# An audio tower on Trainium2: six of the 32 products of a group's states with C on GpSimd instead of VectorE

## The chip, the cores and the metric

One core of a Trainium2 chip runs the whole program. The metric is the device time of one execution in microseconds (us). The engines are TensorE (PE, its weight loads shown as PEld), VectorE (DVE), ScalarE (ACT), GpSimd (POOL) and SyncE (SP, which issues most DMAs). Each takes its own list of instructions in order, and they meet at semaphores only.

## The reference, cut to what matters

The input is 64 sequences of 2 x 4096. A convolution and a projection make h of 64 x 128 tokens x 256; then comes a selective state-space layer on the normalized h, then a mixture of 8 experts, two for each token. The layer, with 512 inner channels d and 16 states n:

```python
xc = silu(conv(x_inner) + conv_b); x_ssm = xc @ W_xproj   # delta_raw, Bm, Cm
delta = softplus(delta_raw * w_dt + b_dt)
dA = exp(delta[..., None] * A)
dBx = delta[..., None] * Bm[:, :, None, :] * xc[..., None]
h = dA_t * h + dBx_t                 # over the 128 tokens of a sequence
y = einsum('bdn,bn->bd', h, c_t)     # states times C, summed over n
y = (y + xc * D_param) * silu(z); out = y @ W_out
```

Everything is computed in float32.

## The kernel before

The 64 sequences are worked in 16 groups of GB = 4, so a tile row has GT = 512 tokens. The 512 inner channels are NCH = 4 chunks of 128 partitions. A group is HU = 32 steps k; step k treats chunk k // 8 and the two states 2 (k % 8) and the next, as one tile of 128 x 1024. The groups run in `steps`: two unrolled, then a loop over pairs (two halves, `par` 0 and 1), then two unrolled. Each engine has a `step` function, whose order over k is written out by hand. After the groups comes the expert part, 136 tiles.

What a step does:
- ACT, `exps` (L726 and L732): writes dA = exp(delta A) into one of two PSUM pairs, `dA[k % 2]`. It may do so when the product of step k - 2 is done. ACT issues the exponentials of step k + 1 in step k, and after them the other work of that step: copies of z (L713), `norm1` of the next group (L655, at k = 3), copies for the next group's input projection and convolution (L667, L675), silu, softplus and others.
- POOL, `make_dbx` (L536): one multiply of 128 x 2048 for two steps, u times B, into one of two buffers. It may start when the scans of the buffer's previous content are done. In between come delta, u, small work for the normalizations (`rsqrt`) and scatters of rows.
- DVE, `scan` (L927): runs the recurrence in place in PSUM over `dA[k % 2]` and dBx. `times_c` (L935): multiplies the states with C (`c_rep`, in SBUF) into one of two SBUF buffers `hc[k % 2]`. In some steps come `gate_y`, `residual`, statistics and the router's small operations.
- PE, `add_state` (L1244): adds the two states' products into the chunk's PSUM bank `yacc` by two matmuls with the identity, after the other matmuls that `step` gives this k. These are the projection of z (k = 0 to 3), the output projection of the former group (`project_out`, L1256, k = 4 to 7), the input projection of the next group (`project_x`, L1190, k = 7, 10, 13, 16) and its convolution in two halves (`conv`, L1215, k = 8 and 9, 11 and 12, 14 and 15, 17 and 18), the small projection to delta, B and C (`x_ssm`, k = 20), transposes, the router, and the embedding of the group after next (`embed`, k = 24 and 25).
- SP: loads B and C of the next group in quarters as the old ones become free, saves `hnew` to DRAM (`save_h`) and loads it back into `hres` for the residual.

Three SBUF tensors of 128 x 1024 matter for the change. `hnew` holds the embedded h of the next group from step 25 until `norm1` has read it at step 3 and `save_h` has stored it. `hres` holds the former group's h from its load at the group's start to `residual` at step 9, and the transposed input (`xt`) at steps 22 to 25. `xn` holds the normalized h from step 3 to the transposes at steps 5 and 6, and the router's input at steps 14 to 16.

Of the kernel before, what the change touches and what calls it, by code (L numbers as in the profile page):

```python
# [5 lines left out]
ALU = mybir.AluOpType  # L6
# [11 lines left out]
def audio_tower(nc, x, W_embed, b_embed, W_proj, b_proj, W_in, conv_w, conv_b, W_xproj, w_dt, b_dt, A_log,  # L18
# [40 lines left out]
    with ExitStack() as ctx:  # L59
# [110 lines left out]
        emb_pair = [bank_a, bank_b]  # L170

        def scratch(i):
            return bank_b[:, (2 + i) * GB * E:(3 + i) * GB * E].rearrange("p (b e) -> p b e", b=GB)
# [61 lines left out]
        scan_done = sem("scan_done")  # L235
        hc_ready = sem("hc_ready")
        skip_done = sem("skip_done")
        sum_done = sem("sum_done")
# [87 lines left out]
        def _(sp):  # L326
# [25 lines left out]
            def load_hres(g, saves):  # L352

                sp.wait_ge(emb_full, 2 * saves)
                apart(sp, "sp")
                sp.wait_ge(h_saved, 16 * saves)
# [15 lines left out]
            def share_ssm(g):  # L372
# [10 lines left out]
                for q in range(NQ):  # L383
                    ahead(sp, dbx_ready, UN * (g - 1) + UN - NQ + q + 1)
                    apart(sp, "sp")
                    spread(flat(b_rep[:, q * QN:(q + 1) * QN, :]), g, 1 + q * QN, QN).then_inc(b_loaded[q], 16)
                    ahead(sp, hc_ready, HU * (g - 1) + HU - HC + 2 * q + 2)
                    apart(sp, "sp")
                    spread(flat(c_rep[:, q * QN:(q + 1) * QN, :]), g, 1 + S + q * QN, QN).then_inc(c_loaded[q], 16)

# [40 lines left out]
            def tail(g):  # L431
                load_hres(g, G)
                free_for(B_AT, (skip_done, NCH * G), (u_ready, NCH * G))
                free_for(C_AT, (dbx_ready, UN * G))
                free_for(C_AT + 2 * QN * GT, (hc_ready, HU * G - 4))
                free_for(X_AT + SCN, (hc_ready, HU * G), (scan_done, HU * G))
                free_for(E * MW)
                store_h2(g)
# [29 lines left out]
        def _(pool):  # L468
# [83 lines left out]
            def second_row(g):  # L552
# [4 lines left out]
                    .then_inc(second_set, 1)  # L557

            def scatter(g, k, b0):
                if b0 == 0:  # L560
# [67 lines left out]
        def _(actq):  # L628
# [7 lines left out]
            def evac_xt(g, m):  # L636
                actq.wait_ge(tx_full, 2 * g + m + 1)
                if m == 0:
                    ahead(actq, h2_ready, 2 * (g - 2))
                nc.scalar.activation(xt[m], bank_a[0:KX, :], ACT.Copy).then_inc(tx_free, 1)  # L640

            def evac_h(g, m):
                actq.wait_ge(emb_full, 2 * g + m + 1)
                if m == 0:
                    ahead(actq, h_saved, 16 * g)
                dst = hnew[:, 2 * m:2 * m + 2, :].rearrange("p b c -> p (b c)")
                nc.scalar.activation(dst, bank_a, ACT.Copy).then_inc(emb_free, 1)

            def norm1(g):

                actq.wait_ge(pow1, g + 1)
                ahead(actq, xnt_full, NK * g)
                ahead(actq, l_full, g - 2)
                for b in range(GB):
# [228 lines left out]
        def _(dve):  # L883
# [36 lines left out]
            def scan(g, k):  # L920
# [5 lines left out]
                src = flat(dBx[(k // 2) % 2][:, 2 * (k % 2):2 * (k % 2) + 2, :])  # L926
                nc.vector.tensor_tensor_scan(h, h, src, 0.0, ALU.mult, ALU.add).then_inc(scan_done, 1)  # L927

            def times_c(g, k):
                j = k % HC  # L930
                dve.wait_ge(scan_done, HU * g + k + 1)
                if k < HC and k % 2 == 0:
                    dve.wait_ge(c_loaded[k // 2], 16 * (g + 1))
                ahead(dve, sum_done, HU * g + k - 1)
                nc.vector.tensor_tensor(flat(hc[k % 2][:, :, :]), flat(dA[k % 2]), flat(c_rep[:, 2 * j:2 * j + 2, :]),  # L935
                                        ALU.mult).then_inc(hc_ready, 1)

            def gate_y(g, c):
                dve.wait_ge(sum_done, HU * g + HC * (c + 1))
                if c == 0:  # L940
# [204 lines left out]
        def _(pe):  # L1145
# [95 lines left out]
            def add_state(g, k):  # L1241
                pe.wait_ge(hc_ready, HU * g + k + 1)
                for i in range(2):
                    last = nc.tensor.matmul(yacc[(k // HC) % 2], ident[:, :], hc[k % 2][:, i, :], start=False,  # L1244
                                            stop=(k % HC == HC - 1 and i == 1))
                last.then_inc(sum_done, 1)
# [68 lines left out]
            def step(g, par, first, second, more, last):  # L1315
                for k in range(HU):
# [136 lines left out]
```

## Time and profile before

| | us |
|---|---|
| median of 3 runs | 3042.44 |
| lowest and highest | 3042.26, 3043.21 |
| the profiled execution | 3046.24 |
| its span, first to last instruction | 3044.5 |
| busy in it: PE, DVE, ACT, POOL | 2628.8, 2162.7, 1469.8, 1729.4 |

The profile is of one execution. The page gives each engine's busy time, then the span in 40 slices (76 us each; a digit is the busy share in tenths). A list of waits says which engine waited for which instruction's result. A timeline lists instructions in order of time: start, duration, engine, line, what is written and read; in brackets stands how long the engine was idle before, and who ended that. Lines are those of the kernel; `psum` in a row can be any of the PSUM banks, `arena` holds xc, B, C and dBx.

### The profile page before, as it was taken

To read this page: it belongs to the slowest core of one execution; us is meant where nothing else is said; L and a number is where in the kernel's file an instruction comes from. 1 tells how busy PE (TensorE), PEld (TensorE's weight loads), DVE (VectorE), ACT (ScalarE), POOL (GpSimd) and SP (SyncE) were. 2 spreads that over 40 slices of the span, in tenths; PEclk is the share of its full clock that TensorE was granted. 3 is DMA by queue.
4 is the path that set the end of the run, shared out by engine and by line. 5 is a ranking of instruction groups with operands and counts; after the bars stand their busy time and mean duration, and the time that the engine had idled before them with its cause. 6 is when DMAs were issued, how large, how long until landed. Compare 5 with 4: busy or idle time off the path is not lost. (4 is left out here: it accounts for less than half of the span.)

```text
span 3044.5 us, 32684 instructions
## 1 busy us (share of the span) xinstructions
PE 2628.8 (86%) x7774; PEld 1299.6 (43%) x7775; DVE 2162.7 (71%) x2367; ACT 1469.8 (48%) x2717; POOL 1729.4 (57%) x864
## 2 busy tenths in 40 slices
PE   4689898888979889897888978887569999999999
PEld 2234343343434334343333434333236666666665
DVE  0599999989999998998999999999632222222222
ACT  2565656656555665665666565665212222222222
POOL 1566767777685767768676676777422222222222
PEclk9899899999999999999999999999879999999999
DMA  1321303223040321303123140321432222222222
GB/s 38 126 101 37 144 27 134 78 75 131 21 145 27 132 92 60 140 16 141 56 103 117 36 144 26 132 86 64 165 80 44 43 45 44 44 44 44 45 44 31
DMA packets 125600, 235.91 MB, mean 77 GB/s; under 512 B 46449, under 2 KB 93714, under 8 KB 109122
## 3 DMA queue, kind: packets, MB, share of 16 engines
q1 hardware_dynamic: 98342, 200.56, 19.2%
q0 software_dynamic: 26128, 34.36, 6.5%
q14 instruction: 77, 0.63, 0.1%
q8 instruction: 17, 0.28, 0.0%
q10 hardware_dynamic: 1036, 0.09, 0.0%
HBM read 182.22 MB, written 53.78 MB: 78 GB/s over the span
## 5 line engine op out<-in xcount | busy, mean ns | idle before, releaser
L536 POOL TENSOR_TENSOR arena<-u,arena 128x2048 f32<-128x2048 f32 x256 | 1157.9, 4528 | 357.2 <-DVE psum L927 355.9
L1244 PE MATMUL psum<-hc,ident 128*128 128x512 f32 x2048 | 1060.8, 645 | 272.6 <-DVE hc L935 272.4
L927 DVE TENSOR_TENSOR_SCAN psum<-psum,arena 128x1024 f32<-128x1024 f32 x512 | 1172.9, 2291 | 124.4 <-ACT psum L732 83.2
L1244 PEld LDWEIGHTS psum<-hc,ident 128*128 128x128 f32 x2048 | 379.7, 200 | 836.6 <-DVE hc L935 485.5
L732 ACT ACTIVATE psum<-delta,a_neg 128x508 f32<-128x508 f32 x1024 | 656.4, 674 | 0.6
L935 DVE TENSOR_TENSOR hc<-psum,arena 128x1024 f32<-128x1024 f32 x512 | 626.0, 1223 | 19.9 <-DVE psum L927 4.8
L615 POOL DMA_INDIRECT out_dram<-hres,tok_id x136 | 211.1, 1552 | 599.4 <-ACT hres L864 550.0
L1375 PE MATMUL psum<-arena,xnt 128*128 x1088 | 516.0, 597 | 0.0
L1129 DVE COPY z<-psum 128x512 f32<-128x512 f32 x136 | 94.1, 692 | 458.0 <-PE psum L1384 458.0
L864 ACT ACTIVATE hres<-psum,tok_w 128x256 f32<-128x256 f32 x136 | 64.3, 473 | 454.4 <-PE psum L1394 447.7
L1394 PE MATMUL psum<-arena,z 128*128 x1088 | 257.1, 379 | 0.9 <-DVE z L1129 0.9
L1190 PE MATMUL psum<-xnt,w_in_sb 128*128 128x512 f32 x512 | 244.6, 601 | 3.1 <-ACT arena L675 1.6
L1394 PEld LDWEIGHTS psum<-arena,z 128*128 128x128 f32 x1088 | 206.6, 190 | 86.8 <-issue 65.7
L1375 PEld LDWEIGHTS psum<-arena,xnt 128*128 128x128 f32 x1088 | 186.5, 191 | 133.0 <-issue 132.0
L1215 PE MATMUL psum<-xi,diag_cw 128*128 128x512 f32 x512 | 239.8, 591 | 0.0
L726 ACT ACTIVATE psum<-zeros 128x8 f32<-128x8 f32 x512 | 87.8, 171 | 240.1 <-DVE hc L935 225.8
L1123 DVE TENSOR_TENSOR z<-psum,xn 128x512 f32<-128x512 f32 x136 | 94.1, 692 | 138.1 <-issue 98.2
L856 ACT ACTIVATE xn<-psum 128x512 f32<-128x512 f32 x136 | 81.2, 597 | 160.3 <-PE psum L1375 160.3
L1256 PE MATMUL psum<-w_out_sb,yz 128*128 128x256 f32 x512 | 129.0, 398 | 29.7 <-DVE h L953 28.9
L564 POOL DMA_INDIRECT expert_rows<-row,slot x128 | 130.0, 1015 | 39.6 <-issue 37.9
L1190 PEld LDWEIGHTS psum<-xnt,w_in_sb 128*128 128x128 f32 x512 | 98.4, 193 | 123.3 <-issue 119.4
L1215 PEld LDWEIGHTS psum<-xi,diag_cw 128*128 128x128 f32 x512 | 96.7, 189 | 123.0 <-issue 123.0
(145 smaller groups left out, 1921.4 us busy)
## 6 DMA issues: line engine op xcount, KB each, us to landing
arena<-ssm_rows SPq DMA_DIRECT2D x128, 1024.0 KB, 5.9
delta<-expert_rows SPq DMA_DIRECT2D x136, 129.0 KB, 2.0
h_saved_rows<-hnew SPq DMA_DIRECT2D x16, 512.0 KB, 6.5
hres<-h_saved_rows SPq DMA_DIRECT2D x16, 512.0 KB
out_dram<-h SPq DMA_DIRECT2D x16, 512.0 KB, 3.0
draw<-ssm_rows SPq DMA_DIRECT2D x16, 256.0 KB, 3.2
arena<-in_L_ffn_wg_dram SPq DMA_DIRECT2D x8, 512.0 KB
arena<-in_L_ffn_wi_dram SPq DMA_DIRECT2D x8, 512.0 KB
```

The source lines that it names most:

```text
L536: pool.tensor_tensor(dBx[k % 2], rep, b_rep[:, q * QN:(q + 1) * QN, :], ALU.mult).then_inc(dbx_ready, 1)
L564: pool.indirect_dma_start(out=rows_dram[:, :], out_offset=bass.IndirectOffsetOnAxis(ap=slot[:, k, b:b + 1], axis=0), in_=row[:, b, :], in_ ...
L615: pool.indirect_dma_start(out=out.rearrange("b o l -> (b o) l"), out_offset=bass.IndirectOffsetOnAxis(ap=tok_id[k][:, 0:1], axis=0), in_=y ...
L732: last = nc.scalar.activation(o, d, ACT.Exp, scale=a_neg[:, c, n:n + 1])
L927: nc.vector.tensor_tensor_scan(h, h, src, 0.0, ALU.mult, ALU.add).then_inc(scan_done, 1)
L935: nc.vector.tensor_tensor(flat(hc[k % 2][:, :, :]), flat(dA[k % 2]), flat(c_rep[:, 2 * j:2 * j + 2, :]), ALU.mult).then_inc(hc_ready, 1)
L1190: last = nc.tensor.matmul(dst, w_in_sb[:, k, c * P:(c + 1) * P], xnt[:, k, :], start=(k == 0), stop=(k == NK - 1))
L1215: last = nc.tensor.matmul(dst, diag_cw[:, c, k, :], xi[c % 2][:, :, k:k + T], start=(k == 0), stop=(k == TAPS - 1))
L1244: last = nc.tensor.matmul(yacc[(k // HC) % 2], ident[:, :], hc[k % 2][:, i, :], start=False, stop=(k % HC == HC - 1 and i == 1))
L1256: last = nc.tensor.matmul(bank_b[:, b * C:(b + 1) * C], yz[:, c, t0:t0 + T], w_out_sb[:, c, :], start=(c == 0), stop=(c == NCH - 1))
L1375: last = nc.tensor.matmul(dst[k % 2], xgt[k % 2][:, q * P:(q + 1) * P], w, start=(q == 0), stop=(q == NK - 1))
L1394: last = nc.tensor.matmul(py[k % 2], actt[k % 2][:, q * P:(q + 1) * P], w, start=(q == 0), stop=(q == NH - 1))
```

## The change

For the steps k = 4, 10, 12, 18, 20 and 26 of each group the scan writes its result into an SBUF tensor instead of PSUM (4, 10 and 18 into `hnew`, 12 into `hres`, 20 and 26 into `xn`), and GpSimd multiplies it there, in place, with C. The products of the other 26 steps stay on DVE. TensorE adds the product of one of the six steps later than before: 4 after 8, 10 after 14, 12 after 16, 18 after 22, 20 after 24, 26 after 30. GpSimd makes a product after the multiply of B numbered 4, 7, 8, 11, 12 and 15. DVE waits before such a scan until the tensor is free (`state_free`); ACT's exponentials may overwrite dA after the scan where the product is one of the six; ACT and SP get waits before they write the three tensors again. `rsqrt` of the second normalization moves from position 5 to 6 on GpSimd.

```diff
+        ON_POOL = {4: hnew, 10: hnew, 12: hres, 18: hnew, 20: xn, 26: xn}
+        DONE_WITH = {8: 4, 14: 10, 16: 12, 22: 18, 24: 20, 30: 26}
+        OWN = [k for k in range(HU) if k not in ON_POOL]
+        NOWN, NPL = len(OWN), len(ON_POOL)
+        SUMS = [k for own in OWN for k in ([own, DONE_WITH[own]] if own in DONE_WITH else [own])]
...
@@ SP: load_hres, share_ssm
+                sp.wait_ge(sum_done, HU * g + nth_sum[12] + 1)
...
+                    for k in (HU - HC + 2 * q, HU - HC + 2 * q + 1):
+                        if k in ON_POOL:
+                            ahead(sp, hc_pool, NPL * (g - 1) + nth_pool[k] + 1)
...
@@ POOL
+            def times_c(g, k):
+                pool.wait_ge(scan_done, HU * g + k + 1)
+                j = k % HC
+                if k < HC:
+                    pool.wait_ge(c_loaded[j // 2], 16 * (g + 1))
+                state = ON_POOL[k][:, :, :].rearrange("p b c -> p (b c)")
+                pool.tensor_tensor(state, state, flat(c_rep[:, 2 * j:2 * j + 2, :]), ALU.mult).then_inc(hc_pool, 1)
...
+                    if k in (4, 7, 8, 11, 12, 15):
+                        times_c(g, {4: 4, 7: 10, 8: 12, 11: 18, 12: 20, 15: 26}[k])
...
-                        if k == 5:
+                        if k == 6:
                             rsqrt(g - 1, 1, stat2, pow2)
@@ ACT: exps
-                ahead(actq, hc_ready, HU * g + k - 1)
+                if k >= 2 and k - 2 in ON_POOL:
+                    actq.wait_ge(scan_done, HU * g + k - 1)
+                elif k >= 2:
+                    actq.wait_ge(hc_ready, NOWN * g + nth_own[k - 2] + 1)
...
@@ DVE: scan
-                nc.vector.tensor_tensor_scan(h, h, src, 0.0, ALU.mult, ALU.add).then_inc(scan_done, 1)
+                if k in ON_POOL:
+                    state_free(g, k)
+                    out_ = ON_POOL[k][:, :, :].rearrange("p b c -> p (b c)")
+                else:
+                    out_ = h
+                nc.vector.tensor_tensor_scan(out_, h, src, 0.0, ALU.mult, ALU.add).then_inc(scan_done, 1)
+
+            def state_free(g, k):
+                known = isinstance(g, int)
+                if k == 4:
+                    dve.wait_ge(xn_ready, min(g + 2, G) if known else g + 2)
+                    dve.wait_ge(h_saved, 16 * (min(g + 2, G) if known else g + 2))
+                if k in (10, 18):
+                    dve.wait_ge(sum_done, HU * g + nth_sum[{10: 4, 18: 10}[k]] + 1)
+                if k == 12:
...
+                        dve.wait_ge(h2_ready, 2 * g)
+                if k == 20:
+                    dve.wait_ge(xnt_full, NK * (min(g + 2, G) if known else g + 2))
+                    ahead(dve, l_full, g)
+                if k == 26:
+                    dve.wait_ge(sum_done, HU * g + nth_sum[20] + 1)
...
             def times_c(g, k):
-                j = k % HC
+                if k in ON_POOL:
+                    return
...
@@ PE: add_state, step
-                pe.wait_ge(hc_ready, HU * g + k + 1)
+                if k in ON_POOL:
+                    pe.wait_ge(hc_pool, NPL * g + nth_pool[k] + 1)
...
-                    add_state(g, k)
+                    if k not in ON_POOL:
+                        add_state(g, k)
+                    if k in DONE_WITH:
+                        add_state(g, DONE_WITH[k])
```

## Rows read from the trace of the kernel before

**Rows 1.** The page, busy time by engine, and DVE in 40 slices of the span
```profile
PE 2628.8 (86%) x7774; PEld 1299.6 (43%) x7775; DVE 2162.7 (71%) x2367; ACT 1469.8 (48%) x2717; POOL 1729.4 (57%) x864
...
DVE  0599999989999998998999999999632222222222
```

**Rows 2.** Timeline of SP's DMA issues, the load of hres, two groups apart (start, duration)
```profile
759.54 0.34 SPq L358 DMA_DIRECT2D hres<-h_saved_rows  x1
...
1022.68 0.33 SPq L358 DMA_DIRECT2D hres<-h_saved_rows  x1
```

**Rows 3.** Waits from 300 to 2000 us, 13 groups: us in total, times, longest
```profile
POOL arena L536 <- DVE psum L927: 283.0, 114, 6.9
PE psum L1244 <- DVE hc L935: 189.5, 165, 2.5
...
ACT arena L675 <- PE psum L1215: 120.0, 39, 5.3
...
DVE psum L927 <- ACT psum L732: 72.9, 71, 2.7
```

**Rows 4.** One group in three windows: busy us of PE, PEld, DVE, ACT, POOL; clock; DMA
```profile
1015.00:1068.70 53.70, 50.46 (x137) 24.52 (x138) 49.16 (x40) 28.89 (x55) 43.15 (x21) 1.00 0.21 62
1068.70:1096.40 27.70, 27.70 (x83) 13.28 (x82) 26.95 (x27) 16.85 (x35) 18.21 (x5) 1.00 0.00 1
1096.40:1146.80 50.40, 35.56 (x86) 12.73 (x86) 45.61 (x47) 34.77 (x57) 34.70 (x23) 0.90 0.45 169
```

**Rows 5.** Instructions by line and form, 300 to 2000 us, GpSimd and DVE
```profile
L536 POOL TENSOR_TENSOR arena<-u,arena 128x2048 f32<-128x2048 f32 x208 | 940.8, 4528 | 284.1 <-DVE psum L927 283.0 <-issue 0.2
...
L520 POOL TENSOR_TENSOR delta<-delta,soft 128x512 f32<-128x512 f32 x52 | 66.0, 1269 | 2.4 <-ACT delta L707 2.4
...
L927 DVE TENSOR_TENSOR_SCAN psum<-psum,arena 128x1024 f32<-128x1024 f32 x415 | 950.9, 2291 | 92.8 <-ACT psum L732 72.9 <-issue 11.2 <-POOL arena L536 7.1
L935 DVE TENSOR_TENSOR hc<-psum,arena 128x1024 f32<-128x1024 f32 x416 | 508.7, 1223 | 16.9 <-DVE psum L927 4.8
```

**Rows 6.** Timeline of DVE: scan, product 4 and scan 5; scans 8, 14, 17, 21
```profile
1030.73 2.30 DVE L927 TENSOR_TENSOR_SCAN psum<-psum,arena 128x1024 f32<-128x1024 f32 x1 [0.77 <-POOL arena L536]
1033.06 1.22 DVE L935 TENSOR_TENSOR hc<-psum,arena 128x1024 f32<-128x1024 f32 x1
1034.21 2.29 DVE L927 TENSOR_TENSOR_SCAN psum<-psum,arena 128x1024 f32<-128x1024 f32 x1
...
1046.41 2.30 DVE L927 TENSOR_TENSOR_SCAN psum<-psum,arena 128x1024 f32<-128x1024 f32 x1 [1.06 <-ACT psum L732]
...
1071.93 2.30 DVE L927 TENSOR_TENSOR_SCAN psum<-psum,arena 128x1024 f32<-128x1024 f32 x1
...
1082.33 2.29 DVE L927 TENSOR_TENSOR_SCAN psum<-psum,arena 128x1024 f32<-128x1024 f32 x1
...
1100.93 2.30 DVE L927 TENSOR_TENSOR_SCAN psum<-psum,arena 128x1024 f32<-128x1024 f32 x1 [0.22 <-ACT psum L732]
```

**Rows 7.** Timeline of ACT: norm1, then the copies of convolutions 0 and 3
```profile
1030.79 2.06 ACT L655 ACTIVATE xn<-hnew,shift,rstd 128x256 f32<-128x256 f32 x4
...
1057.35 0.67 ACT L675 ACTIVATE arena<-psum,cb 128x512 f32<-128x512 f32 x1
...
1093.05 0.69 ACT L675 ACTIVATE arena<-psum,cb 128x512 f32<-128x512 f32 x1 [5.31 <-PE psum L1215]
```

**Rows 8.** Timeline of PE: a projection, convolutions 2 and 3, two sums
```profile
1041.94 1.99 PE L1256 MATMUL psum<-w_out_sb,yz 128*128 128x256 f32 x8 [1.73 <-DVE h L953]
...
1077.74 1.88 PE L1215 MATMUL psum<-xi,diag_cw 128*128 128x512 f32 x4
...
1091.13 1.88 PE L1215 MATMUL psum<-xi,diag_cw 128*128 128x512 f32 x4
1092.85 3.60 PE L1244 MATMUL psum<-hc,ident 128*128 128x512 f32 x8
```

**Rows 9.** Timeline of PE, the same projection in the group before
```profile
910.48 3.08 PE L1256 MATMUL psum<-w_out_sb,yz 128*128 128x256 f32 x8 [2.08 <-DVE h L953]
```

More of the change, by code:

```diff
@@ L170, in audio_tower @@
         emb_pair = [bank_a, bank_b]
+        ON_POOL = {4: hnew, 10: hnew, 12: hres, 18: hnew, 20: xn, 26: xn}
+        DONE_WITH = {8: 4, 14: 10, 16: 12, 22: 18, 24: 20, 30: 26}
+        OWN = [k for k in range(HU) if k not in ON_POOL]
+        NOWN, NPL = len(OWN), len(ON_POOL)
+        nth_own = {k: i for i, k in enumerate(OWN)}
+        nth_pool = {k: i for i, k in enumerate(ON_POOL)}
+        SUMS = [k for own in OWN for k in ([own, DONE_WITH[own]] if own in DONE_WITH else [own])]
+        nth_sum = {k: i for i, k in enumerate(SUMS)}
+        LAST_SUM = [max(nth_sum[k] for k in range(HC * c, HC * c + HC)) for c in range(NCH)]
+        assert len(SUMS) == HU and NOWN % 2 == 0 and not ON_POOL.keys() & {0, 1, HU - 2, HU - 1}
         def scratch(i):
@@ L386, in share_ssm @@
                     spread(flat(b_rep[:, q * QN:(q + 1) * QN, :]), g, 1 + q * QN, QN).then_inc(b_loaded[q], 16)
-                    ahead(sp, hc_ready, HU * (g - 1) + HU - HC + 2 * q + 2)
+                    last = [k for k in (HU - HC + 2 * q, HU - HC + 2 * q + 1) if k not in ON_POOL][-1]
+                    ahead(sp, hc_ready, NOWN * (g - 1) + nth_own[last] + 1)
                     apart(sp, "sp")
+                    for k in (HU - HC + 2 * q, HU - HC + 2 * q + 1):
+                        if k in ON_POOL:
+                            ahead(sp, hc_pool, NPL * (g - 1) + nth_pool[k] + 1)
+                            apart(sp, "sp")
                     spread(flat(c_rep[:, q * QN:(q + 1) * QN, :]), g, 1 + S + q * QN, QN).then_inc(c_loaded[q], 16)
@@ L639, in evac_xt @@
                     ahead(actq, h2_ready, 2 * (g - 2))
+                    ahead(actq, sum_done, HU * (g - 2) + nth_sum[12] + 1)
                 nc.scalar.activation(xt[m], bank_a[0:KX, :], ACT.Copy).then_inc(tx_free, 1)
@@ L645, in evac_h @@
                     ahead(actq, h_saved, 16 * g)
+                    ahead(actq, sum_done, HU * (g - 2) + nth_sum[18] + 1)
                 dst = hnew[:, 2 * m:2 * m + 2, :].rearrange("p b c -> p (b c)")
@@ L652, in norm1 @@
                 ahead(actq, xnt_full, NK * g)
+                ahead(actq, sum_done, HU * (g - 2) + nth_sum[26] + 1)
                 ahead(actq, l_full, g - 2)
@@ L929, in times_c @@
             def times_c(g, k):
[L930 removed]
+                if k in ON_POOL:
+                    return
+                j, n = k % HC, nth_own[k]
                 dve.wait_ge(scan_done, HU * g + k + 1)
[L932 removed]
+                if k < HC and (k % 2 == 0 or k - 1 in ON_POOL):
                     dve.wait_ge(c_loaded[k // 2], 16 * (g + 1))
[L934 to L935 removed]
+                if n >= 2:
+                    dve.wait_ge(sum_done, HU * g + nth_sum[OWN[n - 2]] + 1)
+                else:
+                    ahead(dve, sum_done, HU * (g - 1) + nth_sum[OWN[NOWN + n - 2]] + 1)
@@ L1241, in add_state @@
             def add_state(g, k):
-                pe.wait_ge(hc_ready, HU * g + k + 1)
+                if k in ON_POOL:
+                    pe.wait_ge(hc_pool, NPL * g + nth_pool[k] + 1)
+                    state = ON_POOL[k][:, :, :].rearrange("p (i b) c -> p i (b c)", i=2)
+                else:
+                    pe.wait_ge(hc_ready, NOWN * g + nth_own[k] + 1)
+                    state = hc[nth_own[k] % 2]
+                c = k // HC
                 for i in range(2):
-                    last = nc.tensor.matmul(yacc[(k // HC) % 2], ident[:, :], hc[k % 2][:, i, :], start=False,
-                                            stop=(k % HC == HC - 1 and i == 1))
+                    last = nc.tensor.matmul(yacc[c % 2], ident[:, :], state[:, i, :], start=False,
+                                            stop=(nth_sum[k] == LAST_SUM[c] and i == 1))
                 last.then_inc(sum_done, 1)
```

14 lines of the change are left out of this document (11 added, 3 removed).

## The prediction

> **What bounds the kernel now.** I read the page first: DVE is 9 or 10 tenths busy over the first 28 slices and 2 over the rest, where PE takes over with the expert tiles [rows 1]. The change lies wholly in the first part, 16 groups of 32 steps. Two groups take 263.14 us, 131.6 each [rows 2]. Then the waits of a stretch of 13 groups [rows 3]: PE waits 189.5 us for products of DVE, which looks as if DVE were the bound; but DVE itself waits 72.9 us for the exponentials of ACT, and ACT waits 120.0 us in its copies of the convolution for PE. So the three are one loop: ACT issues in order, exponentials (L732) stand behind copies out of PSUM (L675), and these wait for matmuls that stand in PE's order behind sums (L1244). Last, one group cut in three [rows 4]: in the middle, steps 12 to 20, PE is busy 27.70 us of 27.70, DVE 26.95. PE has idle time before and after it (3.2 of 53.7 and 14.8 of 50.4 us), none in it. That is what I weigh the change against.
>
> **What it takes off DVE.** A product costs 1.22 us, but the next scan starts 1.15 us after the product [rows 5, 6]. Six a group are 6.9 us, 110 us in 16 groups. The scan into SBUF in place of PSUM has no row; both the scan (PSUM out, 2291 ns for 1024 elements) and the product (SBUF out, 1223 ns) exist, and their ratio is that of the two operations, so I leave the scan at 2.29 us and allow 0.1 us either way, six times: 0.6 us a group.
>
> **What it puts on GpSimd.** 1024 elements between 512 in 1.27 us and 2048 in 4.53 us [rows 5]: 2.12 ns an element, 2.35 us (bounds 1.27 and 4.53). Six are 14.1 us a group. GpSimd waited 283.0 us for scans in 13 groups, 21.8 each [rows 3], so it fits; and it runs ahead: a product follows a multiply of B whose scans come later. The one place where it is close is dBx 8 behind product 10: GpSimd starts dBx 7 when scan 11 is done, and 4.5 + 2.35 + 4.5 us later dBx 8 is there, 4 us before scan 16. Product 26 stands ahead of the next group's delta, but that multiply waits for scan 29 anyway. The load of C's second quarter, and those queued behind it on SP, wait for product 26, some 5 us longer; the saved rows of hnew still leave right after the group's last product, and what waits for their landing (the load of hres) was issued 8.0 us before scan 4 (1022.68 against 1030.73 [rows 2, 6]), so scan 4's wait for them ends early. The waits for hres (residual at step 9) and for xn (router at step 16) end well before scans 12 and 20. These cost nothing. The move of the second normalization's rstd by one step on GpSimd costs nothing either: its user on ACT comes at step 12.
>
> **The new wait at step 4.** Scan 4 writes hnew, and must wait until ACT has read it in norm1 (L655). In the trace scan 4 starts at 1030.73 and the pass runs 1030.79 to 1032.85 [rows 6, 7]: 2.2 us, against 1.15 saved right after it. Queued behind this wait are all later scans; scan 5 comes 1.0 us late. Step 6's residual, PE's second projection behind it (which in the trace starts when it ends, 1041.94 [rows 8]), the transpose, ACT's copy and exponential 8 all shift, and scan 8, which already waited for that chain [rows 6], is 0.9 us late.
>
> **The sums that are moved.** I follow one group, scan by scan, each engine in its own order; PE starts its next matmul group 1.72 us after one of four (1091.13 to 1092.85 [rows 8]). The sum of 4 now comes after that of 8, 10 after 14, 12 after 16, 18 after 22, 20 after 24, 26 after 30.
> Sum 4 comes ahead of the second half of convolution 0. Before, its copy ran right behind exponential 10 [rows 7]; now exponential 10 ends at 1058.3, sums 8 and 4 hold PE to 1058.0, the half convolution then takes until 1059.9, and only then come the copy (0.6) and exponential 11 (1.4, its row pair L726 and L732), to 1061.9. DVE, which has no product 10, is ready at 1060.8 and waits 1.2 us: what step 10 saved is gone, still 0.9 late.
> Step 12 saves its 1.15 (scan 13 is 0.3 early). But scan 14 needs product 11, sum 11, convolution 1, its copy, half of norm2 and exponential 14, one after the other, and in the trace this chain ended with no slack at 1071.93 [rows 6]. Nothing in it got shorter: 0.9 late again.
> In the full stretch PE now makes two more sums than before, 10 and 12; their old places fall into waits. Convolution 2's second half, at 1077.74 [rows 8], moves by 0.1 (the start of the stretch), 0.3 (a wait for product 14) and 1.7 (sum 10), 2.2 in all; its copy gates exponential 17, ready just before scan 17 at 1082.33 [rows 6]: 2.1 late. Step 18 saves 1.15: 0.8 to 0.9 late at scan 19. Convolution 3's second half, 1091.13, moves by 2.2 and 1.7 (sum 12), 3.8, to 1094.95; the copy ends at 1097.5 and exponential 20 at 1098.9, where DVE is ready for it before 1097. ACT, which already waited 5.31 us for it [rows 7], issues exponential 20, then silu of xc, then exponential 21 (5.9 us in the trace from the end of exponential 20, all its own work), for which scan 21 waited [rows 6]: 3.8 late. The saving of step 20 is eaten by this wait too. At step 26 DVE saves 1.15 once more, but sum 20 stands ahead of the second embedding matmul, which gates ACT's copy and exponential 27: 3.2, then 3.8 late. Steps 27 to 31 are as before, so the group ends 3.8 us late and the next begins so.
>
> **TensorE's clock.** In the other half of the loop PE had waited 2.08 us for DVE, and its projection then took 3.08 us against 1.99 here [rows 9, 8]; the granted clock over the last part of the group is 0.90 [rows 4], so a part of it runs at 1.2 GHz. Without sum 4 PE idles some 3.1 us at step 5 and 2.2 at step 6, so I expect the slow projection in both halves: 1.1 us in every second group (bounds 0 and 2.2), on the chain to scan 8. A mean of 0.55. By the Trainium skill, "TensorE: Matmul & The Clock Gate", Part 1, an idle array falls to half its clock; this agrees in kind with the row, and the sum goes by the row.
>
> **The sum.** 14 groups with a next and a former one: 14 x (3.8 + 0.55) = 60.9. The first has no projection, rows or router on PE, its stretch is less full: + 2, an estimate between 0 and 3.8. The last has nothing of a next group on ACT and PE: five savings reach the end, - 5.75 (that of step 26 falls into a wait for GpSimd behind its scatters). Sum + 57.2. On the profiled execution (span 3044.5, 3046.24 in all, 1.7 around it) that is 3103.4; the median of the runs shown is 3042.44, 3.8 lower, and the forecast on it is 3099.6 us. The extra waits themselves cost no time I can read; 0.3 us a group is inside the range.
>
> **A rule against the change.** DVE's products take 1.22 us also where GpSimd is in the midst of a multiply (1033.06, with GpSimd busy 43 of 53.7 us [rows 6, 4]), so the rows show no contention. The Trainium skill, "Perfetto Trace Analysis", Optimizing Scalar/DVE Operations, warns that both share a read port, so that moving work between them might not help; "SBUF — State Buffer", Who interferes with whom, confines this to DVE instructions with two inputs in SBUF. The scans keep one input in PSUM, so by the narrower rule it gives nothing, and the trace agrees.
>
> **Rivals.**
> A, faster: DVE alone sets the pace. It keeps 110 us less 2.2 for scan 4 in 15 groups, 33: - 77, 2965 us. It decides if PE can take sums 10 and 12 in steps 12 to 20, that is if 3.4 us of its time there are slack. For it: PE's 189.5 us of waits for DVE. Against: 27.70 busy of 27.70. 0.14.
> B, less slow: norm1 comes as early as scan 4 wants it, since ACT is freed from the wait for products. The group then starts the stretch 2.1 us earlier and loses 1.7: 14 x 1.7 + 2 - 5.75 = + 20, 3062. Against: norm1 stands behind the copy of z, which waits for PE, not for DVE. 0.06.
> C, slower still: scan and product do hold each other up, or GpSimd's 1024 elements cost near 4.53 us. Two such delays of 2.2 us a group, at dBx 8 and step 20, give 14 x 4.4 = 62 more: 3161. Against: the durations in rows 5 and 6. 0.06.
> D, no change: the losses are half of what I find, and equal the savings: within 0.2%, 0.03.
>
> **How the numbers follow.** Forecast 0.71, with its own range: the clock's bounds are -8 and +15, the scan's +-8, and one more or one fewer of the five lost savings +-16: 3070 to 3125. A 0.14, B 0.06, C 0.06, D 0.03. The range that leaves out two in ten takes B and D in, and the near part of C: 3030 to 3140. A measurement of this kernel can tell about 0.2% from no change, 6 us. Faster 0.14 (A), same 0.03, slower 0.83.
>
> **What would show it.** Right: scan 4 waits about 2 us for ACT L655; the wait of L675 for PE grows; DVE's L927 waits for ACT grow from 72.9 to well over 150 us in 13 groups; DVE is busy 117 us less (96 x 1.22) while two groups take some 272; PE has no gap from about step 13 to 18. Wrong: if convolution 3's second half comes no later after product 11 than before, or if PE shows gaps in the stretch, A holds; if products on GpSimd are not near 2.35 us, or products on DVE over 1.3, C.

## The result, and the profile after

The changed kernel takes 3129.86 us (median of 4 runs, 3122.62 to 3135.44) beside 3042.82 us for the kernel before (4 runs, 3042.26 to 3043.66): ratio 1.0285, 95% interval 1.0266 to 1.0304. It is slower by 87 us. The forecast was 3099.6 us with a range of 3030 to 3140.

The page of the changed kernel, busy time by engine and DVE in 40 slices; it answers to [rows 1]:

```profile
PE 2652.8 (85%) x7774; PEld 1319.6 (42%) x7775; DVE 2048.9 (66%) x2271; ACT 1471.2 (47%) x2717; POOL 1950.8 (63%) x960
...
DVE  0588888888888888887888888889922222222222
```

DVE is busy 113.8 us less, GpSimd (POOL) 221.4 us more: the work moved as the change says. PE's 7774 matmuls are the same ones and take 24.0 us more (2652.8 against 2628.8), which fits its lower granted clock, 0.942 over the execution against 0.956. DVE's slices fell from 9 to 8, and there is one more of them: the first part of the kernel is longer though its busiest engine has less to do.

Its waits from 300 to 2000 us, some 12 and a half groups (engine, tile and line, what it waited for: us in total, times, longest); they answer to [rows 3]. Line 970 is the scan, 1002 DVE's product, 555 GpSimd's multiply by B, 1317 the sum, 1282 the convolution, 708 ACT's copy of it, 770 the exponential, 688 norm1:

```profile
POOL arena L555 <- DVE psum L970: 309.9, 120, 7.8
...
PE psum L1317 <- DVE hc L1002: 202.6, 89, 5.5
ACT arena L708 <- PE psum L1282: 188.1, 50, 7.2
DVE psum L970 <- ACT psum L770: 157.7, 104, 4.6
...
DVE hnew L970 <- ACT xn L688: 41.3, 12, 4.1
DVE xn L970 <- ACT psum L770: 35.4, 13, 2.8
```

DVE's waits for exponentials grew from 72.9 to 193 us (157.7 + 35.4), and ACT's in the copy from 120.0 to 188.1, the longest of them from 5.3 to 7.2. The wait of scan 4 for norm1 is new, 41.3 us in 12 groups. All three were in the forecast.

The durations by form in the same stretch, to be read beside [rows 5]:

```profile
L970 DVE TENSOR_TENSOR_SCAN psum<-psum,arena 128x1024 f32<-128x1024 f32 x325 | 744.2, 2290 | 161.1 <-ACT psum L770 157.7 <-issue 2.7
...
L1002 DVE TENSOR_TENSOR hc<-psum,arena 128x1024 f32<-128x1024 f32 x324 | 396.0, 1222 | 10.7 <-DVE psum L970 1.5
...
L585 POOL TENSOR_TENSOR hnew<-hnew,arena 128x1024 f32<-128x1024 f32 x37 | 87.2, 2357 | 0.0
L970 DVE TENSOR_TENSOR_SCAN hnew<-psum,arena 128x1024 f32<-128x1024 f32 x37 | 84.8, 2291 | 42.1 <-ACT xn L688 41.3
```

A product on GpSimd takes 2357 ns (2.35 us was worked out), the scan into SBUF 2291 ns (2.29), and DVE's scans and products are as long as before. So rival C is out: no scan and no product got slower, they only come later.

**One group of after, where the walk said the time would go.** DVE: scans 4, 11, 14, 17, 20 and 21 of the group that starts at 918.71 us (start, duration, idle time before and its releaser):

```profile
936.41 2.29 DVE L970 TENSOR_TENSOR_SCAN hnew<-psum,arena 128x1024 f32<-128x1024 f32 x1 [3.09 <-ACT xn L688]
...
965.33 2.30 DVE L970 TENSOR_TENSOR_SCAN psum<-psum,arena 128x1024 f32<-128x1024 f32 x1 [1.06 <-ACT psum L770]
...
976.20 2.30 DVE L970 TENSOR_TENSOR_SCAN psum<-psum,arena 128x1024 f32<-128x1024 f32 x1 [1.22 <-ACT psum L770]
...
987.76 2.30 DVE L970 TENSOR_TENSOR_SCAN psum<-psum,arena 128x1024 f32<-128x1024 f32 x1 [1.07 <-ACT psum L770]
...
1002.62 2.29 DVE L970 TENSOR_TENSOR_SCAN xn<-psum,arena 128x1024 f32<-128x1024 f32 x1 [2.69 <-ACT psum L770]
...
1008.26 2.30 DVE L970 TENSOR_TENSOR_SCAN psum<-psum,arena 128x1024 f32<-128x1024 f32 x1 [2.02 <-ACT psum L770]
```

What DVE saves by a product that it no longer makes, it waits for an exponential soon after: 1.06 us at scan 11, 1.22 at 14 (product 12), 2.69 at 20 (product 18) and 2.02 at 21. Scan 17 waits too, behind no such product. The reason stands on PE. Its timeline around sums 4, 10 and 12, each ahead of a half convolution:

```profile
959.70 1.88 PE L1317 MATMUL psum<-hnew,ident 128*128 128x512 f32 x4
961.42 1.88 PE L1282 MATMUL psum<-xi,diag_cw 128*128 128x512 f32 x4
...
981.64 1.88 PE L1317 MATMUL psum<-hnew,ident 128*128 128x512 f32 x4
983.36 1.88 PE L1282 MATMUL psum<-xi,diag_cw 128*128 128x512 f32 x4
...
993.31 1.88 PE L1317 MATMUL psum<-hres,ident 128*128 128x512 f32 x4
995.02 1.88 PE L1282 MATMUL psum<-xi,diag_cw 128*128 128x512 f32 x4
```

From 977.41 us to 1002 PE has no gap; a sum of four matmuls holds up the convolution behind it by 1.72 us. ACT then stands in its copy, 3.63 us for convolution 2 and 7.18 us for convolution 3 (5.31 in [rows 7]), with exponentials 17 and 20 queued behind it:

```profile
985.27 0.69 ACT L708 ACTIVATE arena<-psum,cb 128x512 f32<-128x512 f32 x1 [3.63 <-PE psum L1282]
...
1000.37 0.69 ACT L708 ACTIVATE arena<-psum,cb 128x512 f32<-128x512 f32 x1 [7.18 <-PE psum L1282]
```

The same group in three windows (busy us of PE, PEld, DVE, ACT, POOL with counts, clock, DMA), to be read beside [rows 4], which are of the loop's other half:

```profile
918.70:965.30 46.60, 40.78 (x113) 20.27 (x112) 39.16 (x31) 25.12 (x47) 38.82 (x19) 0.96 0.20 64
965.30:1000.20 34.90, 33.35 (x95) 15.43 (x94) 31.65 (x29) 16.73 (x37) 26.64 (x7) 1.00 0.00 0
1000.20:1052.30 52.10, 38.66 (x89) 13.81 (x87) 43.66 (x46) 37.45 (x60) 40.16 (x23) 0.84 0.40 151
```

PE fills the middle (33.35 of 34.90 us), DVE no longer does. In the last part the granted clock is 0.84. Not every group has that: from scan 20 to the next scan 0 it is 0.83 to 0.87 in four of the loop's 12 groups and 0.90 or 0.91 in the others, and 0.90 in all 12 before.

### The profile page after: what moved, and what is told of

The parts are those of the page before. It is cut to its first block and busy times, and to the rows that moved or that the text cites. A ratio compares the mean times of both kernels' runs of the same rounds, so it can differ in the third digit from the quotient of the medians.

```text
span 3120.8 us, 32874 instructions
## 1 busy us (share of the span) xinstructions
PE 2652.8 (85%) x7774; PEld 1319.6 (42%) x7775; DVE 2048.9 (66%) x2271; ACT 1471.2 (47%) x2717; POOL 1950.8 (63%) x960
## 5 line engine op out<-in xcount | busy, mean ns | idle before, releaser
L1317 PE MATMUL psum<-hc,ident 128*128 128x512 f32 x1664 | 880.6, 657 | 281.6 <-DVE hc L1002 280.4
L970 DVE TENSOR_TENSOR_SCAN psum<-psum,arena 128x1024 f32<-128x1024 f32 x416 | 952.4, 2290 | 209.6 <-ACT psum L770 183.8
L1317 PEld LDWEIGHTS psum<-hc,ident 128*128 128x128 f32 x1664 | 322.5, 206 | 728.1 <-DVE hc L1002 417.3
L1002 DVE TENSOR_TENSOR hc<-psum,arena 128x1024 f32<-128x1024 f32 x416 | 508.5, 1222 | 14.6 <-DVE psum L970 1.5
L708 ACT ACTIVATE arena<-psum,cb 128x512 f32<-128x512 f32 x64 | 44.0, 687 | 232.4 <-PE psum L1282 232.4
```

What stands on the lines that cost most here:

```text
L970: nc.vector.tensor_tensor_scan(out_, h, src, 0.0, ALU.mult, ALU.add).then_inc(scan_done, 1)
L1002: nc.vector.tensor_tensor(flat(hc[n % 2][:, :, :]), flat(dA[k % 2]), flat(c_rep[:, 2 * j:2 * j + 2, :]), ALU.mult).then_inc(hc_ready, 1)
L1317: last = nc.tensor.matmul(yacc[c % 2], ident[:, :], state[:, i, :], start=False, stop=(nth_sum[k] == LAST_SUM[c] and i == 1))
```

## The experiments

Each was timed in three rounds beside the kernel before; in the three sets that was 3043.9, 3046.5 and 3045.0 us (medians of 7, 13 and 7 runs). "Late" is how much later a scan starts than in the kernel before, both counted from their group's scan 0, a mean over six groups of one half of the loop. Half 0 is the first group of a pair, where the loop begins anew, half 1 the second, which the prediction walked; where one number stands it is that of half 1. Where no diff is shown, the edit of the changed kernel is that of its two tables, which products go to GpSimd and where (ON_POOL) and behind which sum theirs come (DONE_WITH), with the waits that follow from them.

**1. The order of the sums alone.** DVE makes all 32 products; six go to the idle tensors, and their sums come as late as in the change.

```
-                out_ = ON_POOL[k]...            # scan into the idle tensor
+                out_ = h                        # scan in PSUM as before
 ...times_c on DVE:
+                if k in ON_POOL:
+                    state_free(g, k)            # product 4 waits for norm1
+                    nc.vector.tensor_tensor(ON_POOL[k]..., flat(dA[k % 2]), flat(c_rep[...]), ALU.mult)
```

> All 32 products stay on DVE, made from PSUM; only those of steps 4, 10, 12, 18, 20 and 26 go into the idle tensors, and TensorE adds them as late as in the changed kernel. GpSimd has no product, DVE saves nothing. Theory (the moved sums stand ahead of the convolutions and the embedding, and ACT and the scans wait behind these): walked on the rows of before, scan 17 is 1.4 us later, scan 20 2.6, scan 21 3.3, and steps 26 and 27 add 0 to 1.7; 3.3 to 5.0 us a group, 3085 to 3117 us. Rival (the loss comes from the wait at step 4 and from GpSimd): within 8 us of before, 3043 to 3051.

Measured 3107.14 us, ratio 1.0205 [1.0188, 1.0222]. That is 63 us, without a single product moved. Scan 17 is 2.6 us late, 20 is 3.8, 21 is 4.5: the steps of the walk. In half 0 it is 0.8, 2.3 and 2.7. One thing besides the order is left in it: product 4 goes into hnew, and here it is the product that waits for norm1:

```profile
DVE hnew L993 <- ACT xn L686: 12.3, 11, 1.9
```

But at scan 8 the mean lateness of the two halves is only 0.2 us, and from there to the group's end it grows by 3.6 and 3.7. Nearly all of the 63 us thus arises where only the order of the sums differs. Rival A (DVE sets the pace) is out, since here DVE has all its work and the loss is there.

**2. Without the wait at step 4.** `ON_POOL = {4: soft[:, 0:2, :], 10: hnew, 12: hres, 18: hnew, 20: xn, 26: xn}`

> As the changed kernel, but state 4 goes into the half of soft that is free from the second delta on, so scan 4 doesn't wait for norm1; state 10 is the first in hnew. Theory: scan 5 is 1.15 us early instead of 0.9 late, and all that follows moves by these 2.1 us: 14 x 2.1 = 29 less than the changed kernel's 3130, 3100 us (3090 to 3110). Rival (the sums' place alone sets the time, a wait at step 4 is covered by it): 3125 to 3130.

Measured 3109.48 us, 1.0221 [1.0204, 1.0238], 20 us below the changed kernel (13 between the profiled executions), where 29 were expected. Scan 5 was to be 1.15 us early and is 0.3 late (half 0: 0.8), for it waits longer for exponential 5. Here both, from half 0:

```profile
1204.93 2.30 DVE L971 TENSOR_TENSOR_SCAN psum<-psum,arena 128x1024 f32<-128x1024 f32 x1 [2.08 <-ACT psum L771]
```

```profile
1201.55 2.06 ACT L688 ACTIVATE xn<-hnew,shift,rstd 128x256 f32<-128x256 f32 x4
```

ACT issues exponential 5 right behind norm1, so norm1 holds up scan 5 even where scan 4 doesn't wait for it. At the group's end half 1 has won 1.3 us on the changed kernel, and half 0 nothing (4.1 late against 3.9). It leaves a kernel no faster than experiment 1, which has all products on DVE. 9 us of its time are longer jumps of the loop (experiments 9 and 10), which experiment 1 doesn't have; that left out, six products off DVE buy some 7 us of the 110 in this order.

**3. Without products 4 and 26.** `ON_POOL = {10: hnew, 12: hres, 18: hnew, 20: xn}`, `DONE_WITH = {14: 10, 16: 12, 22: 18, 24: 20}`

> Only the products of steps 10, 12, 18 and 20 go to GpSimd, with sums at 14, 16, 22 and 24; 4 and 26 are as before. Theory: scan 11 and 13 are 1.15 and 2.3 us early, scan 14 1.15, scan 17 on time, scan 21 1.7 us late: 14 x 1.7, + 2 in the first group, - 4.6 in the last, 3064 us. With product 26 on DVE SP's loads of C are not late, and the stall of scan 0 at the loop's end is back at 2 us (2.7 to 4.6 in the changed kernel). Rival (each product moved costs the same): two thirds of the loss, 3100.

Measured 3067.5 us, 1.0076 [1.0059, 1.0093], against 3064 expected. Here the saving of step 10 survives (scan 11 is 1.0 us early), since no sum 4 stands ahead of convolution 0; it is 2.3 early at 13, 1.0 at 14, then 0.1 late at 17 and 1.4 at 20, when sums 10 and 12 have been made. With product 26 back on DVE the loop's jumps take 5.4 to 5.7 us, as in the kernel before.

**4. Sums 10 and 12 behind the last convolution.** `DONE_WITH = {8: [4], 18: [10, 12], 22: [18], 24: [20], 30: [26]}`, product 18 into the first half of soft, the gate of chunk 1 at step 20

> As the changed kernel, but sums 10 and 12 come behind the second half of convolution 3 (step 18), the gate of chunk 1 moves from step 19 to 20, and state 18 goes into soft because hnew is held longer. Theory: the full stretch of TensorE is 3.4 us shorter, scan 17 is 0.9 late in place of 2.1 or more, scan 21 about 0.9 in place of 3.8 or more: 3 us a group less than the changed kernel, 3080 us (3070 to 3092). Rival (the loss comes from step 4, the clock and GpSimd): less than 10 us below 3130.

Measured 3076.31 us, 1.0109 [1.0082, 1.0135], 54 us below the changed kernel with the same six products on GpSimd. The runs scatter from 3069.52 to 3086.93, so the 54 us are known to some 10. Scan 21 is 1.2 to 1.8 us late instead of 3.7 to 4.8. Where these two sums stand is the larger part of the loss.

**5. Four products whose sums stand ahead of nothing urgent.** `ON_POOL = {10: hnew, 14: soft[:, 0:2, :], 16: soft[:, 2:4, :], 22: xn}`, `DONE_WITH = {18: [10, 14], 21: [16], 25: [22]}`, gate 1 at step 20

> Other steps: the products of 10, 14, 16 and 22 go to GpSimd (into hnew, the two halves of soft, xn). Sums 10 and 14 come behind convolution 3's second half (step 18), sum 16 at step 21, sum 22 behind the second embedding matmul (step 25); the gate of chunk 1 is at step 20. No scan waits for norm1. Theory (a product saves its 1.15 us where its sum stands outside TensorE's full stretch and no chain of the other engines ends at the next scan): all four savings are kept, 4.6 us a group, 3044 - 74 = 2970, up to 2995 if the lower clock takes 1.5 us a group. Rival (products on GpSimd do not pay in this loop): 3044 or more.

Measured 2971.33 us (2969.43 to 2978.88), 0.9759 [0.9742, 0.9777]: it beats both kernels. Its waits in the same stretch:

```profile
ACT arena L705 <- PE psum L1274: 83.8, 26, 4.1
DVE psum L968 <- ACT psum L768: 79.1, 71, 2.7
```

ACT waits for convolutions 83.8 us, less than the 120.0 of [rows 3], and DVE's waits for exponentials are near what they were (79.1 beside 72.9). A scan is 1.0 us early at 11, 2.5 at 17, 2.9 at 21, 4.2 at 23, and the next group 4.3 to 4.5.

**6. Two of these.** `ON_POOL = {10: hnew, 22: xn}`, `DONE_WITH = {18: [10], 25: [22]}`

> The same with the products of 10 and 22 alone, sums at 18 and 25. Theory: 2.3 us a group, 3044 - 37 = 3007 (to 3025 with the lower clock). Rival: 3044 or more.

Measured 3029.12 us, 0.9945 [0.9927, 0.9962]: 17 us gained, 39 were expected. Up to scan 25 all is as foreseen (2.3 us early in half 1, 2.6 in half 0); at scan 27 only 0.9 and 0.3 are left. PE's timeline at step 24 of this kernel, a sum and then the embedding's first half and the skip product:

```profile
1108.30 2.68 PE L1304 MATMUL psum<-hc,ident 128*128 128x512 f32 x4 [3.30 <-DVE hc L989]
1110.91 2.07 PE L1230 MATMUL psum<-hres,w_eff 45*128 45x512 f32 x2
1112.90 2.07 PE L1293 MATMUL psum<-arena,diag_d 128*128 128x512 f32 x2
```

and its windows, the idle time, the sum, and what follows (the clock is the third number from the end):

```profile
1105.00:1108.30 3.30, 0.00 (x1) 0.00 (x1) 3.27 (x3) 1.07 (x3) 3.23 (x5) 1.00 0.79 268
1108.30:1110.90 2.60, 2.60 (x4) 0.67 (x4) 2.57 (x2) 1.37 (x3) 2.60 (x1) 0.72 0.15 63
1110.90:1114.90 4.00, 4.00 (x6) 1.46 (x6) 3.96 (x3) 1.73 (x3) 3.50 (x4) 0.50 0.09 33
```

The same windows and the embedding of the kernel before:

```profile
1110.43:1112.90 2.47, 0.00 (x0) 0.00 (x0) 2.44 (x3) 0.59 (x1) 1.20 (x1) 0.94 0.51 206
1112.90:1116.40 3.50, 3.47 (x5) 1.21 (x5) 3.46 (x3) 1.39 (x3) 3.33 (x2) 0.55 0.00 0
1116.40:1118.40 2.00, 2.00 (x6) 0.76 (x6) 2.00 (x1) 0.79 (x2) 1.70 (x2) 1.00 0.18 64
```

```profile
1116.37 1.12 PE L1176 MATMUL psum<-hres,w_eff 45*128 45x512 f32 x2
```

Both kernels go to 1.2 GHz here after PE has idled for 2.5 and 3.3 us. Before, the low clock (0.55) falls on the sum alone, and the embedding runs at 1.00, in 1.12 us. Here it falls (0.50) on the embedding and the skip product, 2.07 us each. ACT's copy of the embedding, which waited 3.50 us for it, and exponential 26 behind the copy come late.

That this is the clock's doing, the groups of this one execution show. PE idles 3.2 to 3.3 us before that sum in each of the loop's 12 groups. In eight the embedding's first half then takes 2.07 us, and scan 27 is between 0.4 us early and 0.8 late, after 2.2 to 2.4 early at scan 25. In three it takes 1.54 to 1.58 us, and 0.7 us is lost. In one it takes 1.12 us as in the kernel before, and the saving is kept (2.4 early at 25, 2.5 at 27):

```profile
1628.79 3.41 PE L1304 MATMUL psum<-hc,ident 128*128 128x512 f32 x4 [3.30 <-DVE hc L989]
1632.13 1.12 PE L1230 MATMUL psum<-hres,w_eff 45*128 45x512 f32 x2
```

What makes one group differ from the next, the runs don't show.

**7. A later load, in the kernel before.** The changed kernel loses 1.8 us on average at each of the loop's five jumps back (below). A suspect was the load of C's second quarter, which now waits for product 26.

```
-                    ahead(sp, hc_ready, HU * (g - 1) + HU - HC + 2 * q + 2)
+                    ahead(sp, hc_ready, HU * (g - 1) + HU - HC + 2 * q + (3 if q == 1 else 2))
```

> The kernel before, with one edit: the load of the second quarter of C waits for the product of step 28 in place of 27, about when product 26 of GpSimd lets it go in the changed kernel. Theory (the late load crowds the loads and the saving of hnew into the moment when the loop jumps back, and the first scan of the next pair of groups waits longer for the engines to go on): scan 31 to scan 0 grows from 5.5 us to 7 or 8 at the six jumps, + 11, 3055 us. Rival (the longer jump comes from elsewhere in the change, the program's length say): 5.5 us as before, 3044 us within 2.

Measured 3044.23 us (10 runs), 0.9996 [0.9986, 1.0005]: no effect, and the jumps stay at 5.4 to 5.6 us. The expectation failed. The edit had not done what it was made for: from 1143.5 to 1145.5 us, just before the jump's scan 0 at 1146.07, the DMA engines were at a share of 0.41, so the load was still over in time. That needed a stronger version, experiments 9 and 10.

**8. The four products with early sums.** `DONE_WITH = {14: [10], 17: [14], 20: [16], 25: [22]}`, all else as in 5, gate 1 at 19

> The four products of the experiment with 10, 14, 16 and 22, but their sums inside the full stretch: 10 at 14, 14 at 17, 16 at 20, 22 at 25, and the gate at 19 again. Theory: two sums more stand ahead of convolution 3's second half, 3.4 us, which takes back three of the four savings: scan 21 about on time, only 22 kept: 3044 - 16 = 3028 (3020 to 3045), 45 to 60 us slower than with the late sums. Rival (the place of the sums does not matter once no scan waits for norm1): the same time as with the late sums.

Measured 3008.39 us, 0.9873 [0.9857, 0.989]. The same four products take 37 us more, by the place of three sums and of the gate that waits for them. The kernel is still faster than expected (3028): scan 21 is 1.1 us early and scan 23 2.4 us, so the savings of steps 14 and 16 are lost, but those of 10 and 22 are not. I had forecast that the early sums would take that of 10 too.

A part of the 37 us is TensorE's clock again. In five of the 12 groups the embedding's first half takes 2.07 us, and scan 27 is 0.6 to 0.7 us late; in the other seven it takes 1.12, and scan 27 is 3.8 to 4.0 early. Experiment 5 has three such slow groups, which end about 2.4 us worse than its others. By these differences, an estimate, the clock makes some 15 of the 37 us.

**9. The load later still, in the kernel before.** As 7, with `(4 if q == 1 else 2)`

> The kernel before, with one wait changed: the load of C's second quarter, and the loads queued behind it on SP, wait for the product of step 29 rather than 27, so that they start some 6 us later and are still moving data while the loop jumps back. Theory (the jump is slower when the DMA engines are full during it): the time from scan 31 to the next scan 0 at the five jumps grows from 5.4 to 5.65 us to 6.3 or more, 5 x 1 to 2 us = 3048 to 3053 us, and the window of the jump shows a DMA share near 1. Rival (the jump is slower for another reason, such as the product of step 26 on GpSimd or a longer program): the jumps stay at 5.4 to 5.65 us and the time at 3043 to 3046.

Measured 3062.36 us, 1.0058 [1.0041, 1.0075], 17 us slower from one wait of a load. All five jumps take 8.06 to 8.44 us, from scan 31 to the next scan 0, against 5.40 to 5.65: 13.5 us of the 17. The rest falls inside the groups. The windows over one jump (start:end, length, busy us of PE, PEld, DVE, ACT, POOL, clock, DMA share, GB/s), first of this kernel, with scan 0 of the next group:

```profile
1152.50:1154.50 2.00, 2.00 (x4) 0.97 (x4) 2.00 (x1) 1.29 (x3) 1.84 (x2) 0.50 1.02 418
1154.50:1156.50 2.00, 1.65 (x4) 0.51 (x4) 1.30 (x2) 0.00 (x0) 1.65 (x5) 0.94 1.00 418
1156.50:1158.50 2.00, 2.00 (x6) 0.87 (x5) 0.00 (x0) 0.80 (x3) 1.82 (x3) 1.00 1.00 422
```

```profile
1160.34 2.30 DVE L927 TENSOR_TENSOR_SCAN psum<-psum,arena 128x1024 f32<-128x1024 f32 x1 [4.51 <-issue]
```

then of the kernel before:

```profile
1141.30:1143.30 2.00, 1.86 (x4) 0.68 (x4) 2.00 (x2) 1.39 (x3) 1.84 (x2) 1.00 0.97 397
1143.30:1145.30 2.00, 0.52 (x2) 0.30 (x2) 1.52 (x2) 0.00 (x0) 1.65 (x5) 1.00 0.69 291
1145.30:1147.30 2.00, 2.00 (x6) 0.90 (x5) 0.44 (x1) 1.05 (x3) 1.82 (x3) 1.00 0.69 205
```

DVE waits 4.51 us there for nothing that the profile shows (2.01 in the kernel before), while the DMA engines are full. The size was missed (3048 to 3053 expected): the overlap is longer than in the changed kernel, and the jump dearer.

**10. The load earlier, in the changed kernel.** GpSimd's product 26 goes ahead of its last multiply by B: `{4: 4, 7: 10, 8: 12, 11: 18, 12: 20, 14: 26}` in place of `15: 26`

> The changed kernel, with GpSimd's product 26 put ahead of its last multiply by B (dBx 15) and no longer behind it, so that it ends some 5 us earlier and C's second quarter is loaded that much earlier; the sum of 26 stays where it is. Theory (DMA traffic over the jump): the jumps go back to 5.4 to 5.7 us, the load ends before them, and the time is some 9 us less than the changed kernel's 3129.9: 3120 (3113 to 3126). Rival (it is the product itself or the program's length): the jumps stay at 6.3 to 8.2 us and the time at 3130 or more.

Measured 3120.29 us (3119.46 to 3121.66), 1.0251 [1.0234, 1.0268], 9.6 us below the changed kernel, with all jumps at 5.50 to 5.57 us. The windows over a jump of the changed kernel, then of this one:

```profile
1182.50:1184.50 2.00, 2.00 (x4) 0.85 (x4) 2.00 (x2) 1.39 (x3) 1.84 (x2) 0.50 0.79 332
1184.50:1186.50 2.00, 2.00 (x6) 0.91 (x5) 1.49 (x2) 0.00 (x0) 1.65 (x5) 0.86 1.00 422
1186.50:1188.50 2.00, 2.00 (x6) 0.94 (x5) 0.00 (x0) 0.60 (x2) 1.82 (x3) 1.00 1.06 352
```

```profile
1181.60:1183.60 2.00, 1.95 (x6) 0.90 (x6) 2.00 (x2) 1.39 (x3) 1.84 (x2) 1.00 1.03 426
1183.60:1185.60 2.00, 2.00 (x6) 0.84 (x5) 1.52 (x2) 0.00 (x0) 1.65 (x5) 1.00 0.56 229
1185.60:1187.60 2.00, 2.00 (x6) 0.90 (x5) 0.42 (x1) 1.23 (x3) 1.82 (x3) 1.00 0.72 160
```

The product on GpSimd and the program's length are the same; only the product's place, and with it the traffic, moved. With experiment 9, which moves the traffic alone, this settles that the traffic over the jump is what makes it longer. In both long jumps the granted clock is 0.50 at first, which is not the cause: in experiment 1 it is 0.50 from 1178 to 1182 us, over such a jump, with the DMA share falling to 0.54, and the jump takes 5.4 us. One reserve: between the two profiled executions only 2.7 us of the 9.0 won at the jumps reach the last scan, the rest being lost again in other groups; it is the medians that differ by 9.6.

**11. Six products, sums where there is room.** `ON_POOL = {10: hnew, 12: hres, 14: soft[:, 0:2, :], 16: soft[:, 2:4, :], 20: hnew, 22: xn}`, `DONE_WITH = {18: [10, 12, 14], 21: [16], 23: [20], 25: [22]}`

> Six products on GpSimd again, but at steps 10, 12, 14, 16, 20 and 22, into hnew, hres, the two halves of soft, hnew again and xn, and with their sums where PE has room: 10, 12 and 14 at step 18, 16 at 21, 20 at 23, 22 at 25. Theory (only place decides: each product taken off DVE is worth 1.15 us where its sum stands ahead of nothing that is waited for, and the sum of 20 at step 23 fills the idle time of PE behind which its clock fell): four products gave 4.5 us a group, two more give up to 2.3 us, less about 1 us where scan 20 waits for the sum of 10: 2950 us (2935 to 2972). Rival (PE's total of sums in steps 10 to 20 decides, as in the changed kernel): the third sum at step 18 delays scans 20 and 21, nothing is gained over four products or some is lost: 2975 to 3010.

Measured 2972.36 us (2971.28 to 2974.57), 0.9766 [0.9749, 0.9782]: neither. It equals the four products of experiment 5. The fifth saving is made (2.4 us early at 13) and lost at once (1.0 at 14), at the chain of convolution 1 that already had no slack before; the sixth, of step 20, goes in the wait of scan 21. At scan 23 it is still 0.5 us ahead of experiment 5 (0.9 in half 0), and at 26 no longer; that isn't the clock, as the embedding takes 1.12 us in all 12 groups, and its cause stays open. A product is worth 1.15 us only where the next scan is not held by an exponential.

## Why the prediction was right, and where not

The direction and the mechanism held; the time was 30 us above the forecast, inside the range. The sum, term by term, from the scans of the two profiled executions (the last scan starts at 2180.56 before and at 2257.11 after, + 76.6, against + 57.2 forecast):

- **The walk of a group.** Forecast 3.8 us and 0.55 for the clock in each of 14 groups, 60.9. Measured, without the jumps, 63.0, or 4.5 a group. The mean lateness of the two halves at the scans of the walk is 1.1 at scan 8 (0.9 + 0.55 forecast), 1.2 at 11 (1.45), 2.4 at 17 (2.65), 3.8 at 20 (3.65), 4.3 at 21 (4.35), 4.5 at 27 (4.35). Scan 4 starts 2.1 us late at least, as said.
- **The clock's share of it.** The size was near, the pattern wrong. The projection of step 6 was to be slow in every group instead of every second one. In the trace after it takes 2.4 to 3.8 us in nine of the 14 groups and 1.99 in five, in both halves (before: 3.0 to 3.2 in six, 1.99 in eight). Groups 3 and 7, counted from 0, have it fast in both kernels, and they show the walk without the clock: 0.7 us late at scan 8, 1.8 at 17, 3.2 at 20, 3.7 at 21, 3.9 at 27, where the walk had 0.9, 2.1, 3.1, 3.8 and 3.8. Groups 6 and 8, where it is fast only after, end 2.5 late; the six where it is slow only after (2, 5, 9, 11, 13, 14) end 4.8 to 6.0 late. So the 0.6 between 3.9 and the mean of 4.5 is put down to the clock, an estimate, beside 0.55 forecast. That the sum of such groups comes out at the forecast is in part luck.
- **The first group.** Forecast + 2, measured + 6.7. The step that failed is "its stretch is less full": scan 17 is 1.8 us late there, 20 is 3.9 and 21 is 4.6, as in every other group, and step 26 adds 2.1 more. An estimate between 0 and 3.8 was put in the place of a walk.
- **The last group.** Forecast - 5.75, measured - 2.6. Its savings show from step 10 to 21 (scan 10 is 2.9 us late, scan 21 2.1 early) and at 26, but it had first been made late. There is no norm1 in this group; scan 4 waits 0.94 us and scan 6 1.28 us for multiplies by B, product 8 waits 1.23 us for a sum, and scan 10 0.16. None of these waits is there before. I had counted only what is absent on PE and ACT, and not these waits for GpSimd and for the sums.
- **The jump of the loop.** Not in the forecast: 9.2 us, 1.8 at each of five jumps on average (0.8 to 2.8). The prediction followed this very load ("some 5 us longer") and put it at nothing, as it asked only who waits for its data. Its data were in time. What it cost was DMA traffic over the moment when the engines go back to the loop's start; experiments 9 and 10 show it from both sides.
- **The executions.** The profiled one of after is 7.2 us under its median, where that of before was 3.8 over: 11 us of the 30 are this alone. The forecast allowed for the second, and could not for the first. The changed kernel scatters over 13 us, the kernel before over 1.4 beside it and over 6.6 in the set of 13 runs. The version with early product 26 scatters over 2.2, which would fit the jumps as the source; but experiments 5, 6 and 8, whose jumps are as short, scatter over 8 to 10 us. Where the scatter comes from stays open.

57.2 + 2.1 + 4.7 + 3.2 + 9.2 is 76.4, and with 11.0 for the executions the forecast of 3099.6 becomes 3129.8.

One number of the forecast's range doesn't follow from its own terms: 0 to 2.2 us in every second of 14 groups is 15.4 us at most, 7.7 above the mean, not 15. It changes nothing in the outcome.

Of the rivals, A falls with experiments 1 and 2 (in this order six products more or less on DVE hardly change the time) and with PE's unbroken stretch, C with the durations, B since scan 4 does wait for norm1. Even without that wait only a part of B's gain is there (experiment 2). What A had right is shown by experiments 5 and 11: DVE's time is worth something, 4.4 us a group for four products, but only after the sums have left the stretch in which PE is full, and not beyond four products.

The rule on the shared port, from the Trainium skill, "Perfetto Trace Analysis", Optimizing Scalar/DVE Operations, warns that work moved between these two engines might not help, as they share a read port. The rows after show 1222 and 2290 ns on DVE with GpSimd 221 us busier, so it did not bind here, with one input of DVE's scans and products in PSUM. That the change didn't help has another reason, the order of the sums. The prediction's narrower rule, from the Trainium skill, "SBUF — State Buffer", Who interferes with whom, has a second case there that it left out, DVE instructions in a two-port mode; the equal durations show no sign of that either.

## What to carry to other kernels

Work taken off the busiest engine shortens nothing if the work that it leaves elsewhere is queued, in order, ahead of what the busiest engine waits for next: here sums of 1.72 us ahead of half convolutions and of the embedding made the larger part of a loss of 87 us, where four products whose sums stood behind them gained 75. So place the deferred half first (find the gap of its engine, behind the last instruction that somebody waits for), and choose then which items to move. And of a transfer that moves, ask not only who needs its data but what else runs at that moment: at this loop's jump full DMA engines cost 1.8 to 2.7 us each time on average.

## What the runs showed of the hardware that I had not expected

- The jump of the loop leaves DVE idle for 1.9 to 2.1 us with the DMA engines partly free (share 0.56 to 0.72 in the last two windows above), and for 2.7 to 4.6 us (changed kernel) and 4.5 to 4.9 us (experiment 9) with them full (share 1.00 and more). In the jump shown ACT idles 3.9 us in place of 3.4. The page lists two DMA queues of the kind "instruction"; whether it is their packets that come late over the jump, the runs don't show.
- Idle time won on PE can be lost to its clock, and not in every group: after the same 3.2 to 3.3 us of idle time in experiment 6 the embedding took 2.07 us in eight groups, 1.54 to 1.58 in three and 1.12 in one. In the changed kernel the projection into dt, B and C takes 6.26 us in the group shown, after 3.56 us of idle time, at a granted clock of 0.57. Over 15 groups with that same idle time it takes 6.26 us in two, 5.1 to 5.3 in nine and 3.62 in four; before, it takes 3.62 us in all of them, after 1.85 at most.
- The scan costs the same into SBUF as into PSUM, 2.29 us for 1024 elements, and GpSimd's product with both inputs in SBUF 2.36 us, beside DVE's 1.22.
